# ViT block with attention and eight experts on one core: the attention pipeline's drain in an order of its own, its last second norms in pairs, and expert weights at 1.6 pieces a step

## What is computed

```python
h = tok(x, W)                                     # 2304 x 768 @ 768 x 192
h = h + attn(layernorm(h), W_attn, b_attn, W_o, b_o)
z = layernorm(h)
probs = softmax(z @ router_w.T)
top_w, top_i = top_k(probs, 2)
top_w = top_w / top_w.sum(-1)
for e in range(8):
    w_e = sum(top_w * (top_i == e))
    g = gelu(z @ w1[e] + b1[e], approximate=False)     # 192 -> 768
    out = out + w_e * (g @ w2[e] + b2[e])              # 768 -> 192
h = h + out
```

## Time and profile before

| | |
|---|---|
| median of 3 runs | 415.99 us (414.44 to 416.58) |
| the profiled execution | 412.6 us, span of the instructions 410.5 us |
| busy: TensorE, VectorE, ScalarE, GpSimd | 371.7, 255.7, 212.4, 171.2 us |
| TensorE's granted clock, mean | 0.979 of 2.4 GHz |
| DMA | 42.82 MB, 104 GB/s |

### The profile page before, as it was taken

The page is one execution under the profiler, slowest core; times in us unless marked ns, Lnnn a source line. Parts: engine busy times, 40 slices in busy tenths (PEclk is TensorE's granted clock), DMA queues, the critical chain, the costliest instruction groups (busy, mean ns, idle before and its releaser), DMA issues.

```text
span 410.5 us, 14839 instructions
## 1 busy us (share of the span) xinstructions
PE 371.7 (91%) x5722; PEld 328.0 (80%) x5722; DVE 255.7 (62%) x662; ACT 212.4 (52%) x431; POOL 171.2 (42%) x214
## 2 busy tenths in 40 slices
PE   4989999989999999997998889999999999999910
PEld 4989989979889899874453589999999999999800
DVE  4687468887877778785299255555455554455426
ACT  5668577778778786853210154444444444444400
POOL 8117322346455452317300545555555555553310
PEclk9999999999999999999999999999999999999965
DMA  8973004433334323361151203131322312222058
GB/s 261 350 222 140 17 21 128 133 97 92 102 116 118 86 81 95 107 186 34 51 136 45 52 28 96 55 88 53 88 57 82 85 55 88 59 54 47 30 208 331
DMA packets 29673, 42.82 MB, mean 104 GB/s; under 512 B 12384, under 2 KB 19408, under 8 KB 29608
## 3 DMA queue, kind: packets, MB, share of 16 engines
q1 hardware_dynamic: 25480, 33.37, 26.7%
q0 software_dynamic: 4128, 8.50, 7.6%
HBM read 30.23 MB, written 9.67 MB: 97 GB/s over the span
## 4 chain that ended last, share of the span: by engine, by line
PE 40%; DVE 6%; issue 6%; POOL 3%; DMA 3%; ACT 1%; SPq 0%; POOLq 0%; DVEq 0%
PE PSA L1240 19%; PE PSA L1255 15%; PE PSA L1124 2%; DMA W2h<-yrows 2%; POOL XF L473 2%; PE PSA L1259 2%; PE PSA L1207 2%; DVE PTR L920 1%; DVE H L987 1%; POOL REG L480 1%; DVE VB L918 1%; DMA yrows<-KBR 1%; DVE VB L914 1%; POOL REG L479 1%; SPq L440 0%
## 5 line engine op out<-in xcount | busy, mean ns | idle before, releaser
L1240 PE MATMUL PSA<-YT,W1h 128*128 128x128 f16 x774 | 78.0, 219 | 1.9 <-DVE YT L949 1.9
L1240 PE MATMUL PSA<-YT,W1l 128*128 128x128 f16 (+1 forms) x516 | 75.3, 220 | 0.0
L1255 PE MATMUL PSA<-W2h,PTR 128*128 x516 | 71.0, 246 | 0.3 <-DVE PTR L679 0.3
L510 POOL DMA_INDIRECT yrows<-KBR x43 | 43.0, 999 | 63.7 <-DVE KBR L964 63.7
L1240 PEld LDWEIGHTS PSA<-YT,W1h 128*128 x774 | 63.7, 98 | 6.0 <-DVE YT L949 2.2
L665 ACT ACTIVATE PTR<-PSA 128x768 f32<-128x768 f32 x43 | 34.8, 810 | 63.2 <-PE PSA L1240 63.2
L1255 PE MATMUL PSA<-W2l,PTR 128*128 x258 | 63.6, 246 | 0.0
L505 POOL DMA_INDIRECT REG<-xrows,KBR x43 | 42.4, 985 | 42.8 <-DVE KBR L941 26.6
L670 ACT ACTIVATE PTR<-PTR 128x768 f16<-128x768 f32 x43 | 36.3, 844 | 44.4 <-PE PSA L1259 44.3
L679 DVE SCALAR_TENSOR_TENSOR PTR<-PTR 128x768 f16<-128x768 f32 x43 | 41.2, 959 | 25.5 <-ACT PTR L670 25.5
L964 DVE TENSOR_SCALAR KBR<-PSA,KBR 128x192 f32<-128x192 f32 x43 | 18.0, 418 | 53.1 <-PE PSA L1259 53.1
(11 more groups left out here) (164 smaller groups left out, 793.8 us busy)
## 6 DMA issues: line engine op xcount, KB each, us to landing
WSTG<-w SPq DMA_DIRECT2D x16, 384.0 KB, 3.4
WSTG<-w SPq DMA_DIRECT2D x16, 336.0 KB, 3.2
REG<-xt SPq DMA_DIRECT2D x12, 324.0 KB, 5.1
W1l<-xt SPq DMA_DIRECT2D x10, 324.0 KB, 6.6
VB<-VP SPq DMA_DIRECT2D x99, 19.1 KB
H<-hrows SPq DMA_DIRECT2D x6, 288.0 KB, 2.8
xrows<-REG SPq DMA_DIRECT2D x1, 1600.5 KB
hrows<-H SPq DMA_DIRECT2D x1, 1296.0 KB
```

What stands on the lines that cost most here:

```text
L510: gp.indirect_dma_start(out=yrows, out_offset=bass.IndirectOffsetOnAxis(ap=TARGET[:, s:s + 1], axis=0), in_=YO[s % 2], in_offset=None).the ...
L1240: ins = nc.tensor.matmul(bank(2 * u + f // (FC // 2), 128, FC // 2 * ST_)[:, w:w + ST_], weights[a, c], YT[0:rows, at:at + ST_], start=k = ...
L1255: nc.tensor.matmul(bank(4 + u, ST_, C), GP[a][:, at:at + ST_], weights[b], start=(f, a, b) == (0, 0, 0), stop=False)
```

## The change

- Weight pieces go at 8/5 a step: `pieces(i)` has 1, 2, 1, 2, 2 pieces in turn and ends with step 19; before 1, 2 in turn and the end in step 21.
- The steps after 20 are written out in an order of their own on each engine. The second norm of tiles 0 to 15 stays in step t + 5; tiles 16 to 21 go in three pairs after tile 21's projection.
- A pair has one high-half operation, two low-half operations, six transposes, one eviction, ten router products and one logit copy. GpSimd makes the rows of tiles 16 and 17 and the low halves of the first two pairs; VectorE makes the rows of tiles 18 to 21 (`late_rows`) and the low halves of the last pair (`last_low`).
- Banks: norm pairs in banks 0, 2, 0, the projection of tile 20 in bank 5, the router of tiles 15 to 21 in bank 3.
- Fillers are laid out anew; the stores of H wait for the residuals (`h2_done`), no more for the rows of the norm.

The diff, cut to these parts:

```diff
+        def pair_source(t):
+            return XF[1] if t != PAIRS[1][0] else XF[0]
+
+        def pair_bank(t):
+            return 2 if t == PAIRS[1][0] else 0
...
-            return range(max(0, 3 * i // 2), min(2 * PIECES, 3 * (i + 1) // 2))
-
-        FIRST_NORM, GROUP, DRAIN = 8, 4, 3
+            return range(max(0, 8 * i // 5), max(0, min(2 * PIECES, 8 * (i + 1) // 5)))
+
+        FIRST_NORM, GROUP = 8, 4
+        PAIRED = NT - 6
+        PAIRS = [(t, t + 1) for t in range(PAIRED, NT, 2)]
...
-            at = {t: t + 5 for t in range(NT)}
-            at.update({t: NT - 1 + (t - (NT - 6)) // 2 for t in range(NT - 6, NT)})
-            return [t for t in range(NT) if at[t] == i]
+            return [i - 5] if 5 <= i < PAIRED + 5 else []
...
+        def project_bank(t):
+            return 5 if t == NT - 2 else 6
+
+        def router_bank(t):
+            return 3 if t >= PAIRED - 1 else 6
...
-            for i in range(-2, NT + 1):
+            for i in range(-2, NT):
...
-                sp.wait_ge(n2_row, b)
+                sp.wait_ge(h2_done, b)
...
+            def pair_low(t):
+                gp.wait_ge(n2_hi, t + 2)
+                x = pair_source(t).rearrange("p (t c) -> p t c", c=C)
+                nc.gpsimd.tensor_tensor(pair_rows(t, C, CB), x[:, :, CA:C], pair_rows(t, CA, CB), ALU.subtract).then_inc(n2_lo, 2)
+                nc.gpsimd.tensor_tensor(pair_rows(t, LOW_A, CA), x[:, :, 0:CA], pair_rows(t, 0, CA), ALU.subtract).then_inc(n2_lo, 2)
...
-            for i in range(-6, NT + DRAIN):
+            def pair_low(t):
+                gp.wait_ge(n2_hi, t + 2)
+                x = pair_source(t).rearrange("p (t c) -> p t c", c=C)
+                nc.gpsimd.tensor_tensor(pair_rows(t, C, CB), x[:, :, CA:C], pair_rows(t, CA, CB), ALU.subtract).then_inc(n2_lo, 2)
+                nc.gpsimd.tensor_tensor(pair_rows(t, LOW_A, CA), x[:, :, 0:CA], pair_rows(t, 0, CA), ALU.subtract).then_inc(n2_lo, 2)
+
+            for i in range(-6, NT):
...
+            for t in PAIRS[0]:
+                norm2_row(t)
+            pair_low(PAIRS[0][0])
+            pair_low(PAIRS[1][0])
...
+            def pair_hi(t):
+                if t == PAIRS[0][0]:
+                    act.wait_ge(n2_row, t + 2)
+                else:
+                    act.wait_ge(late_row, t + 2 - PAIRS[1][0])
+                nc.scalar.activation(pair_rows(t, 0, C), pair_source(t).rearrange("p (t c) -> p t c", c=C), ACT.Copy).then_inc(n2_hi, 2)
+
+            def pair_out(t):
+                act.wait_ge(n2_mm, t + 2)
+                act.wait_ge(r_mm, t)
+                nc.scalar.activation(XT[:, :], bank(pair_bank(t), 128, 6 * TT, F16), ACT.Copy).then_inc(n2_done, 2)
+
+            for i in range(NT - 1):
                 step(i)
+            exps(NT - 1)
+            norm2_out(PAIRED - 1)
+            probs_hi(NT - 1)
+            y_hi(NT - 2)
+            inverse_deviation(group(NT - 3))
+            y_hi(NT - 1)
+            pair_hi(PAIRS[0][0])
+            inverse_deviation(group(NT - 1))
+            pair_hi(PAIRS[1][0])
+            pair_out(PAIRS[0][0])
+            pair_hi(PAIRS[2][0])
+            pair_out(PAIRS[1][0])
+            pair_out(PAIRS[2][0])
...
+                if t < NT - 2:
+                    need(dve, o_mm, t + 2)
+                nc.vector.scalar_tensor_tensor(htile(t), bank(project_bank(t), TT, 512)[:, PROJ:PROJ + C], 1 / S_XW, htile(t), ALU.mult, ALU.add).then_inc(h2_done, 1)
...
+            def late_rows(t):
+                dve.wait_ge(rs_done, group(t) + 1)
+                if t == PAIRS[1][0]:
+                    dve.wait_ge(n1_hi, NT)
+                    dve.wait_ge(n1_lo, NT)
+                else:
+                    dve.wait_ge(n2_hi, t - 2)
+                    dve.wait_ge(n2_lo, 2 * (t - 2))
+                for n in range(2):
+                    x = pair_source(t)[:, n * C:(n + 1) * C]
+                    nc.vector.tensor_scalar(x, htile(t + n), MEAN[:, NT + t + n:NT + t + n + 1], RS[:, NT + t + n:NT + t + n + 1],
+                                            ALU.subtract, ALU.mult).then_inc(late_row, 1)
+
+            def last_low(t):
+                dve.wait_ge(n2_hi, t + 2)
+                x = pair_source(t).rearrange("p (t c) -> p t c", c=C)
+                nc.vector.tensor_tensor(pair_rows(t, C, CB), x[:, :, CA:C], pair_rows(t, CA, CB), ALU.subtract).then_inc(last_lo, 1)
+                nc.vector.tensor_tensor(pair_rows(t, LOW_A, CA), x[:, :, 0:CA], pair_rows(t, 0, CA), ALU.subtract).then_inc(last_lo, 1)
...
-            for i in range(NT + DRAIN):
+            for i in range(NT - 1):
                 step(i)
+            for n in pieces(NT - 2):
+                piece_lo(n)
+            shift(NT - 1)
+            residual(NT - 3)
+            outputs(NT - 2)
+            stats2(NT - 3)
+            probs_lo(NT - 1)
+            logits(PAIRED - 1)
+            y_lo(NT - 2)
+            variances(group(NT - 3))
+            outputs(NT - 1)
+            refine(group(NT - 3))
+            y_lo(NT - 1)
+            residual(NT - 2)
+            stats2(NT - 2)
+            residual(NT - 1)
+            stats2(NT - 1)
+            variances(group(NT - 1))
+            late_rows(PAIRS[1][0])
+            refine(group(NT - 1))
+            late_rows(PAIRS[2][0])
+            last_low(PAIRS[2][0])
+            for t, _ in PAIRS:
+                pair_logits(t)
...
+            def pair_transpose(t):
+                if t == PAIRS[2][0]:
+                    pe.wait_ge(last_lo, 2)
+                else:
+                    pe.wait_ge(n2_lo, 2 * (t + 2))
+                pe.wait_ge(qh_done, NT)
+                pe.wait_ge(kh_done, 2 * NT)
+                pe.wait_ge(sub_done, NT)
+                if t == PAIRS[2][0]:
+                    pe.wait_ge(n2_done, PAIRS[1][0])
+                for m in range(2):
+                    for n, at in enumerate(BLOCKS):
+                        ins = nc.tensor.transpose(bank(pair_bank(t), 128, 6 * TT, F16)[:, (3 * m + n) * TT:(3 * m + n + 1) * TT],
+                                                  rows2(t + m, at, 128), IDH[0:TT, 0:TT])
+                ins.then_inc(n2_mm, 2)
+
+            def pair_router(t):
+                pe.wait_ge(n2_done, t + 2)
+                pe.wait_ge(lg_done, t)
+                for m in range(2):
+                    for k, (a, c, n) in enumerate(ROUTER_PRODUCTS):
+                        ins = nc.tensor.matmul(bank(router_bank(t), TT, 512)[:, ROUT + m * E:ROUT + (m + 1) * E],
+                                               two(XT, t + m, 3 * TT)[:, n * TT:(n + 1) * TT],
+                                               WR[a][:, c * E:(c + 1) * E], start=k == 0, stop=k == len(ROUTER_PRODUCTS) - 1)
+                ins.then_inc(r_mm, 2)
...
+            scores(NT - 1)
+            project(NT - 3)
+            outputs(NT - 2)
+            norm2_transpose(NT - 1, PAIRED - 1)
+            unread(1)
+            transpose_probs(NT - 1)
+            transpose_y(NT - 2)
+            router(NT - 1, PAIRED - 1)
+            unread(3)
+            outputs(NT - 1)
+            project(NT - 2)
+            unread(2)
+            transpose_y(NT - 1)
+            unread(3)
+            project(NT - 1)
+            unread(11)
+            pair_transpose(PAIRS[0][0])
+            unread(4)
+            pair_router(PAIRS[0][0])
+            pair_transpose(PAIRS[1][0])
+            unread(1)
+            pair_transpose(PAIRS[2][0])
+            pair_router(PAIRS[1][0])
+            unread(1)
+            pair_router(PAIRS[2][0])
```

57 lines of the change are left out of this document (34 added, 23 removed).

## The result

The change is slower by a little: 419.57 us median of 16 runs against 416.23 of 16 runs of the kernel before, ratio 1.0069 [1.0044, 1.0093]; a second measurement of both gave 419.06 against 417.42, ratio 1.0037 [1.0002, 1.0071]. The ratios in this document, with their 95% intervals, are those of the record and not the quotients of the medians beside them. The second interval only just leaves out no change. Predicted were 412.3 us and a range of 409.0 to 416.8.

The account below looks back on a forecast made before the run. TensorE bounds the steady part, and the drain's chain delays routing one for one. Drain -8.3, weight rhythm +1.0 +1.2 +2.4, sum -3.7 us: median 415.99 to 412.3 us, range 409.0 to 416.8.

Parts of the forecast that it names:

- the wait in step 20: Step 19's second weight piece lands late behind nine value copies; ScalarE stands 3.8 us, TensorE's transposes start late: +2.4 us.
- rival 3: TensorE's clock falls in the new wait between steps 19 and 20: +3.3, 419.3 us, or about 0; chance 0.14.
- Part 3: Weight pieces at 1.6 a step: +1.0 for steps 5 and 17, +1.2 for step 9, +2.4 for step 19.
- Part 1: Drain's first half, last scores to last residual: 15.0 us before, 9.3 after, gain 5.7, as norms no longer precede y.
- Part 2: Last residual to the logits and routing: 10.4 us before, 7.8 after, gain 2.6, with the last norms in pairs.
- The drain, 17.1 us: Last scores to routing, parts 1 and 2 together: from 25.4 to 17.1 us, -8.3 us.
- Rival 1: The weights arrive in time and ScalarE never stands in steps 9 and 19: -6.8, 409.2 us; chance 0.15.
- Rival 2: VectorE's four late rows cost GpSimd's 1.0 each or wait for its port: +2.9, 415.2 us; chance 0.17.
- Rival 4: Rival 2 together with late weight landings at steps 4, 9 and 19: +2.5, 418.5 us; chance 0.07.
- the second piece of step 4: Its fetch goes out at once, some 3.3 us before ScalarE wants it, and lands in time: no ScalarE idle.
- the 1.5 us: In the drain, by the SBUF port rule, VectorE's new rows would wait for GpSimd's low halves, some 1.5 us in all.

Follow-up runs that it names:

- the second execution: The change, unedited, profiled a second time: this execution took 416.83 us; that measurement's median 419.06 us, ratio 1.0037 to the kernel before.
- the best kernel: New drain with the old weight rhythm, plus ten more unread matmuls and the low halves of tiles 18 to 21 on VectorE, against the kernel before: 409.95 us, ratio 0.9843.
- planted: The kernel before with one more subtraction of a weight piece's size on VectorE in steps 5, 9 and 17, into unread memory: 419.66 us, ratio 1.0079.
- the old-rhythm kernel: The change's new drain with weight pieces back at 1, 2 a step, against the kernel before: 413.23 us, ratio 0.9935.
- the first execution: The change's first profiled execution, nothing edited: 422.51 us; that measurement's median 419.57 us, ratio 1.0069 to the kernel before.

## Why the prediction was wrong

**The failed step is the price of the wait in step 20: "+2.4", with the clock's part put at nothing.** The wait was found, at its place, for its reason and at its size (TensorE predicted 2.4, measured 2.47 and 2.53; ScalarE 3.8, measured 4.0 and 4.1). The forecast took it that the clock outlives it; its reason, in rival 3, was that matmuls stand right before and behind. They do not save it: the clock fell to 1.2 GHz 1 to 2 us after TensorE had gone back to work, and stayed there for 7 to 10 us. That was rival 3, given 0.14 and 419.3 us. That the time came to 419.57 and 419.06 is luck in part: its clock term, +7 us, was twice too dear. The drain's first half measured 3.4 more in the second execution (13.4 us from 183.15 to the residual at 196.55, against 10.0 at full clock in the best kernel) and 2.2 more in the first; terms that were too small, below, made up for it. From the first scores to the routing the second execution is 5.2 us over the forecast: these 3.4 us, and 0.7 and 1.1 of parts 1 and 2.

The terms one by one, against the second execution:

- *Part 3, the rhythm, +4.6:* measured 134.27 - 129.62 = +4.65, but with other shares. The second piece of step 5 gives TensorE's steps 5 and 6 +0.23 for 0.5, that of step 9 its step 10 +1.02 for 1.2, that of step 17 its step 18 +0.27 for 0.5, and step 20 has +3.1 for 2.4 (the wait of 2.5, and matmuls at half clock). The second piece where it is alone, planted, costs 0.57 to 0.78 and not 0.5; in the change some of it is won back, and the wait of 0.26 us for the exponential in step 6 is indeed gone.
- *Part 1, the drain's first half, 9.3 us:* 10.0 with the clock up (178.27 to 188.27 in the best kernel): 0.7 short.
- *Part 2, residual to routing, 7.8 us:* 8.75 in the first and 8.9 in the second execution: 1.0 to 1.1 short. The deviations took 3.5 for 3.0 (0.54 of it is two small operations stretched, L763 and L766), the rows 0.67 and 0.78 a pair for 0.6, and each router pass 0.8 for 0.65; ScalarE's high half, the low halves and the evictions came as predicted.
- *The drain, 17.1 us:* 18.6 to 19.6 in the kernels whose clock stayed up in it, and 20.98 and 22.30 as it ran. The gain of "-8.3" is at most -6.8; the best kernel has -6.2 in its profile and -1.57% (6.4 us) in its time.
- *What the sum has not at all* is the clock in the pairs. The new drain, with few fillers between its pairs, has waits of 0.5 to 0.8 us in a row, and the old-rhythm kernel shows what they cost without any late landing: 2.1 us between the routing and the experts and 1.1 in the drain (20.61 against 19.55 with the fillers).

With the terms as measured at full clock the change would be about -6.4 + 4.2 = -2 us, the milder end of the forecast. This is an estimate, from a drain of 19.0 us and from the second execution's +4.65 us less 0.45 for the end of step 20 at half clock. No run shows it: the one with the long waits filled is nearest, and came to +1.1 us with a longer step 10 and two other falls. With the clock it is +1.6 to +3.3.

**The rivals.** Rival 1, weights in time: refuted, the landing wait is there in every profile of this rhythm with three slots, and four slots remove it (1.6%). Rival 2, the pairs give half back: in part. VectorE's rows do not cost GpSimd's 1.0 us each, but beside GpSimd's low halves the small operations of the deviations take 0.34 and 0.52 us, where they take 0.16 elsewhere, and in the old-rhythm kernel GpSimd's wide one takes 1.45 for 0.67 beside VectorE's. Rival 4, landings later still: no, ScalarE's wait in step 19 came within 0.3 us of the working. The prediction saw none at the second piece of step 4; the first execution has one of 0.20 us.

The page "SBUF — State Buffer" of the Trainium skill (section "SBUF: two separate sides") has one of the two engines block the other for a whole instruction. The trace agrees in kind in both directions, at 0.1 to 0.8 us each; the 1.5 us that the prediction worked out by that rule were about 0.6 in the first execution (0.18, 0.36 and 0.11 over the usual lengths) and 0.8 in the second, since the first pair of VectorE's rows found GpSimd idle. The Trainium skill's page "VectorE: DVE Perf Modes" (section "The perf-mode tier table") would have the rows at double rate. They took 0.67 for two, more than the 0.6 taken from the residual's row, so the trace does not show it.

## What to carry to other kernels

A new wait on TensorE has two prices: its length, which a trace of before gives well, and the clock behind it, which needs its own term: here 2 to 4 us for one wait of 2.5 us, about as much again as the wait itself. Before taking a faster order, look at the ring of slots that it draws on: here 1.6 pieces a step with double steps in a row needed one slot more than 1.5 with single and double in turn, and the fetch that stands behind a long batch on the same queue is the one to look at. And when fillers are taken out of a drain, look for the waits at their new places; ten matmuls that nobody reads gave 0.6% here.

## What the runs showed of the hardware

- TensorE's granted clock falls to 1.2 GHz behind one wait of 2.3 to 2.5 us among busy stretches (in all four profiles in which TensorE stood that long), and in some executions at one of 0.66 us, behind one of 0.46 us or behind a row of 0.5 to 0.8 us waits; the kernel before had one of 1.17 us, at 188.91, and none. It came back 3 to 10 us later, with TensorE mostly busy.
- The same kernel with the same waits has falls at different places in different executions. One profile of a kernel says where a fall can come, and not that it does: the planted subtraction's kernel, of 419.66 us median, had none in its profile, while the mean granted clock of most of its other runs was lower.
- Nine copies issued by one queue take 7.4 to 8.5 us of it. A 336 KB fetch behind them was used 3.5 to 4.0 us after its issue in the five profiles with this wait, and a 384 KB one 3.4 to 3.7 us after.
